# Choosing the experts ahead of the second softmax, splitting all expert weights in the value stage, and weighting the expert outputs as they are added

## What is computed

```
logits = jnp.mean(x, axis=1) @ Wr + br                    # one row per image
routing_weights = jax.nn.softmax(logits, axis=-1)
scale = jnp.where(expected_loads > capacity, capacity / expected_loads, 1.0)
routing_weights = jax.nn.softmax(routing_weights * scale, axis=-1)
top_w, top_i = jax.lax.top_k(rw_tok, K)                   # the same for every token of an image
top_w = jax.nn.softmax(top_w, axis=-1)
h = jax.nn.gelu(jnp.einsum('nd,edf->enf', xf, W1) + b1[:, None, :], approximate=False)
y = jnp.einsum('enf,efd->end', h, W2) + b2[:, None, :]
out = jnp.einsum('ne,end->nd', w_dense, y).reshape(B, S, D)
out = _layer_norm(out + x, gamma, beta)
```

## Time and profile before

| what | value |
|---|---|
| time, median of 3 runs | 410.57 us (410.19 to 412.47) |
| span of the profiled execution, first to last instruction | 408.4 us |
| own time of the profiled execution | not given apart from its span; the median lies 2.2 us above the span |
| mean granted TensorE clock | 0.995 |
| busy: PE, DVE, ACT, POOL | 391.0, 311.4, 279.5, 116.5 us |
| shares of the chain that ended last | PE 83%, DVE 7%, ACT 4%, issue 3%, DMA 2% |

### The profile page before, as it was taken

How to read it: one execution, slowest core, us unless ns; L and a number is a source line. 1 busy time by engine, 2 the same in 40 slices (tenths; PEclk the granted TensorE clock), 3 DMA queues, 4 the chain that set the end, 5 groups by cost and what they waited for, 6 DMA issues and landing times.

```text
span 408.4 us, 5562 instructions
## 1 busy us (share of the span) xinstructions
PE 391.0 (96%) x1887; PEld 302.0 (74%) x1892; DVE 311.4 (76%) x699; ACT 279.5 (68%) x530; POOL 116.5 (29%) x113
## 2 busy tenths in 40 slices
PE   8899898999999999999999899999999999998994
PEld 3579895688777888888886688888887766645772
DVE  3798935768888988988899798898899265557745
ACT  1566654558598888888877788888888201457980
POOL 8200004440430730332132063574320000224015
PEclk9999999999999999999999999999999999999999
DMA  7990000000000000000000180000000000000002
GB/s 274 383 312 2 2 2 0 1 2 0 2 1 0 2 0 1 2 1 2 0 0 2 71 343 2 0 0 2 1 1 2 0 2 0 0 2 1 0 2 103
DMA packets 5262, 15.51 MB, mean 38 GB/s; under 512 B 690, under 2 KB 1906, under 8 KB 4978
## 3 DMA queue, kind: packets, MB, share of 16 engines
q1 hardware_dynamic: 4802, 14.19, 9.3%
q10 hardware_dynamic: 432, 0.97, 0.6%
HBM read 14.08 MB, written 1.08 MB: 37 GB/s over the span
## 4 chain that ended last, share of the span: by engine, by line
PE 83%; DVE 7%; ACT 4%; issue 3%; DMA 2%; DVEq 0%; SPq 0%; ACTq 0%
PE ps L1066 13%; PE ps L1068 13%; PE ps L1067 13%; PE ps L1050 13%; PE ps L1162 7%; PE ps L970 2%; PE ps L1002 2%; PE ps L1009 2%; DMA xq<-laid_x_queries 2%; DVE nmax_all L1520 2%; PE ps L827 2%; PE ps L936 2%; PE ps L912 2%; PE ps L959 1%; PE ps L990 1%
## 5 line engine op out<-in xcount | busy, mean ns | idle before, releaser
L706 ACT ACTIVATE exps<-ps,nmax_all 128x1024 bf16<-128x1024 f32 x128 | 142.8, 1115 | 32.5 <-DVE diag_all L1525 32.0
L1520 DVE TENSOR_REDUCE nmax_all<-ps 128x1 f32<-128x1024 f32 x128 | 156.6, 1224 | 7.1 <-PE ps L1068 5.5
L1066 PE MATMUL ps<-qT_hi,kT_hi 128*128 128x512 f32 x256 | 104.7, 409 | 2.2 <-ACT a_rows L723 1.1
L1068 PE MATMUL ps<-qT_hi,kT_lo 128*128 128x512 f32 x256 | 99.8, 390 | 0.0
L1067 PE MATMUL ps<-qT_lo,kT_hi 128*128 128x512 f32 x256 | 99.7, 390 | 0.0
L1066 PEld LDWEIGHTS ps<-qT_hi,kT_hi 128*128 128x128 f32 x256 | 48.1, 188 | 15.6 <-ACT exps L706 1.8
L1050 PE MATMUL ps<-xn,wqkv 128*128 128x342 f32 (+3 forms) x256 | 58.2, 379 | 0.0
L1067 PEld LDWEIGHTS ps<-qT_lo,kT_hi 128*128 128x128 f32 x256 | 48.1, 188 | 10.8 <-issue 0.2
L1068 PEld LDWEIGHTS ps<-qT_hi,kT_lo 128*128 128x128 f32 x256 | 48.0, 188 | 10.3
L487 POOL CAST qT_hi<-xq 128x1024 fp32r<-128x1024 f32 x15 | 15.6, 1040 | 132.5 <-ACT xq L696 132.5
L1050 PEld LDWEIGHTS ps<-xn,wqkv 128*128 128x128 f32 x256 | 42.6, 189 | 11.6 <-issue 1.2
(11 more groups left out here) (216 smaller groups left out, 560.2 us busy)
## 6 DMA issues: line engine op xcount, KB each, us to landing
xs_first<-a_store SPq DMA_DIRECT2D x4, 512.0 KB, 5.4
xs_second<-a_store SPq DMA_DIRECT2D x4, 512.0 KB, 8.3
wqkv<-laid_qkv_weights SPq DMA_DIRECT2D x1, 1536.0 KB, 6.2
wvT<-laid_qkv_weights_T SPq DMA_DIRECT2D x1, 1536.0 KB, 9.5
xq<-laid_x_queries SPq DMA_DIRECT2D x2, 512.0 KB, 6.2
xk<-laid_x_keys SPq DMA_DIRECT2D x2, 512.0 KB, 7.8
x<-in_x SPq DMA_DIRECT2D x1, 1024.0 KB, 12.5
w<-in_L_ffn_W SPq DMA_DIRECT2D x1, 1024.0 KB
```

The lines of the kernel that those rows point to most:

```text
L706: a.activation(exps[:, n % 2, :], slot(job_slot(("score", u, n))), ACT.Exp, bias=nmax_all[:, col:col + 1], accum_out=sum_all[:, col:col + ...
L1066: mm(tgt, keys_hi, qT_hi[:, u % 2, at], start=True, stop=False)
L1068: last = mm(tgt, keys_lo, qT_hi[:, u % 2, at], start=False, stop=True)
L1520: v.tensor_reduce(nmax_all[:, col:col + 1], slot(place), AX_X, ALU.max, negate=True)\
```

## The change

Five things are changed.

- The router takes `max` and `max_index` from the scaled weights, ahead of the second softmax, whose order is the same. The second softmax goes on with its maximum taken from `max`. The gates are made from a hyperbolic tangent of half the difference; the Gelu table is loaded before it.
- POOL splits W1 and W2 of all eight experts in the value stage, once the score job two from the end is done: two copies and two subtractions of 128 x 2048 each. The room is that of tensors no longer needed (`x`, `wqkv`).
- After the indices POOL copies, for each pair, the first bias, hi and lo of W1, hi and lo of W2 and the second bias. `second_layer` on DVE goes.
- W2 no longer carries the gate. Each step's output has a bank of its own (three in turn) and DVE adds it as bank times gate plus running sum, eight times in place of four.
- The gated second bias is added to the tokens by POOL, chunk by chunk, after its copies; DVE's first addition of a chunk waits for it.

```diff
@@ pool, between the attention units and xn_lo @@
+            pool.wait_ge(ffn_in, 64)
+            pool.wait_ge(job_ps, len(JOBS) - 2)
+            pool.wait_ge(w2_centred, E)
+            g.tensor_copy(w1_all_hi[:, :, :], w1[:, :, :]).then_inc(w_rounded, 1)
+            g.tensor_copy(w2_all_hi[:, :, :, :], w2[:, :, :, :]).then_inc(w_rounded, 1)
+            pool.wait_ge(w_rounded, 2)
+            g.tensor_tensor(w1[:, :, :], w1[:, :, :], w1_all_hi[:, :, :].bitcast(F32), ALU.subtract)\
+                .then_inc(w_rounded, 1)
+            g.tensor_tensor(w2[:, :, :, :], w2[:, :, :, :], w2_all_hi[:, :, :, :].bitcast(F32), ALU.subtract)\
+                .then_inc(w_rounded, 1)
+            pool.wait_ge(w_rounded, 4)
...
+            pool.wait_ge(xs_used, UNITS)
+            pool.wait_ge(t1_beta, 2)
+            pool.wait_ge(b2_centred, 1)
             pool.wait_ge(idx_ready, 2)
...
-                    g.tensor_copy(w1_hi[:, b, k, :], chosen).then_inc(w1_ready, 1)
-                    pool.wait_ge(w1_ready, 2 * n + 1)
-                    g.tensor_tensor(w1_lo[:, b, k, :], chosen, w1_hi[:, b, k, :].bitcast(F32), ALU.subtract)\
-                        .then_inc(w1_ready, 1)
+                    g.tensor_copy(b1s[:, b, k, :], b1_all[:, bass.ds(e, 1), :].rearrange("p o f -> p (o f)"))\
+                        .then_inc(b1_ready, 1)
+                    for table, to in ((w1_all_hi, w1_hi), (w1, w1_lo)):
+                        g.tensor_copy(to[:, b, k, :], table[:, bass.ds(e, 1), :].rearrange("p o f -> p (o f)"))\
+                            .then_inc(w1_ready, 1)
+                    for table, to in ((w2_all_hi, w2_hi), (w2, w2_lo)):
...
+                    g.tensor_copy(b2s[:, b, k:k + 1], b2c[:, bass.ds(e, 1)]).then_inc(b2_ready, 1)
+            pool.wait_ge(b2_ready, 2 * TOPK)
+            pool.wait_ge(gates_ready, TOPK)
+            for k in range(TOPK):
+                g.tensor_tensor(b2g[:, :, k], b2s[:, :, k], rs_[:, 10 + k, :], ALU.mult).then_inc(b2_scaled, 1)
+            pool.wait_ge(b2_scaled, TOPK)
+            step(g.tensor_tensor(b2sum[:, :], b2g[:, :, 0], b2g[:, :, 1], ALU.add))
+            for c in range(4):
+                at = slice(c * 512, (c + 1) * 512)
+                g.tensor_scalar(xn[:, at], xn[:, at], b2sum[:, c // 2:c // 2 + 1], None, ALU.add).then_inc(xn_biased, 1)
@@ act, router @@
+            load_table(ACT.Gelu)
             act.wait_ge(r_in, 3)
-            a.activation(rs_[:, 8, :], rs_[:, 7, :], ACT.Exp).then_inc(r_exp, 1)
-            load_table(ACT.Gelu)
+            a.activation(rs_[:, 8, :], rs_[:, 7, :], ACT.Tanh, scale=0.5).then_inc(r_exp, 1)
...
-                act.wait_ge(w2_ready, 4 * (b * TOPK + k) + 1)
+                act.wait_ge(b1_ready, b * TOPK + k + 1)
@@ pe @@
-            for signal, count, times in ((r_exp, 2, 6), (r_in, 2, 4), (r_exp, 4, 4), (idx_ready, 2, 6)):
+            for signal, count, times in ((r_exp, 2, 6), (r_in, 2, 2), (idx_ready, 2, 6)):
...
-                pe.wait_ge(w2_ready, 4 * (b * TOPK + k) + 4)
-                if k == 0 and c >= 2:
-                    pe.wait_ge(LN[2]["centred"], c - 1)
+                pe.wait_ge(w2_ready, 2 * (b * TOPK + k) + 2)
+                if n >= 3:
+
+                    pe.wait_ge(first_added if (n - 3) % 2 == 0 else LN[2]["centred"], (n - 3) // 2 + 1)
@@ dve @@
-            softmax_input(rt[:, 5, :, :], 3)
-            softmax_output(4, 6, 7, 4)
...
+                v.max(rt[:, 8, b, :], rt[:, 5, b, :]).then_inc(dve_step, 1)
...
+            v.tensor_scalar(rs_[:, 3, :], rt[:, 8, :, 0], -1.0, None, ALU.mult).then_inc(r_in, 1)
...
+                v.max_index(top_i[:, b, :], rt[:, 8, b, :], rt[:, 5, b, :]).then_inc(idx_ready, 1)
...
-            second_layer(0)
...
+            def add_output(n):
+
+                c, k = n // 2, n % 2
+                at = slice(c * 512, (c + 1) * 512)
+                dve.wait_ge(y_ps, n + 1)
+                if k == 0:
+                    dve.wait_ge(xn_biased, c + 1)
+                else:
+                    dve.wait_ge(first_added, c + 1)
+                v.scalar_tensor_tensor(centred[:, at], bank(y_bank(n)), rs_[:, 10 + k, c // 2:c // 2 + 1],
+                                       (centred if k else xn)[:, at], ALU.mult, ALU.add)\
+                    .then_inc(LN[2]["centred"] if k else first_added, 1)
+
+            dve.wait_ge(gates_ready, TOPK)
             hidden_remainder(0)
             hidden_remainder(1)
-            second_layer(1)
...
+            for n in range(8):
+                if n == 6:
                     reciprocals(2, 0)
-                residual(c)
...
+                add_output(n)
+                if n + 2 < 8:
+                    hidden_remainder(n + 2)
             reciprocals(2, 1)
```

More of the change, by code:

```diff
@@ L120, in build @@
         head_sel = sb("head_sel", [9 * HEADS, HEADS, P], BF16)
-        x = sb("x", [P, N])
+        with ExitStack() as before_attention:
+            x = before_attention.enter_context(nc.sbuf_tensor("x", [P, N], F32))
+        w1_all_hi = sb("w1_all_hi", [P, E, FF], F32R)
         conv_wT = sb("conv_wT", [P, 3, C])
@@ L135, in build @@
         bqkv = cols[:, NROWS:NCOLS].rearrange("p (j h) -> p j h", j=3)
-        wqkv = sb("wqkv", [P, HEADS, 3, D])
+        with ExitStack() as attention_weights:
+            wqkv = attention_weights.enter_context(nc.sbuf_tensor("wqkv", [P, HEADS, 3, D], F32))
+        w2_all_hi = sb("w2_all_hi", [P, E, FC, D], F32R)
+        w1_lo = sb("w1_lo", [P, 2, TOPK, FF], F32R)
         bqkv_q = sb("bqkv_q", [P, 3, HEADS])
@@ L238, in build @@
         b2s = sb("b2s", [P, 2, TOPK])
+        b2g = sb("b2g", [P, 2, TOPK])
         hid = conv_o[:, :].rearrange("p (n f c) -> p n f c", n=2, f=FC)
@@ L1254, in outputs @@
                     pe.wait_ge(h_lo, 2 * n + f + 1)
-                    tgt = bank(4 + c % 2)
-                    mm(tgt, w2_hi[:, b, k, f, :], hid_hi[:, n % 2, f, :], start=(k == 0 and f == 0), stop=False)
+                    tgt = bank(y_bank(n))
+                    mm(tgt, w2_hi[:, b, k, f, :], hid_hi[:, n % 2, f, :], start=f == 0, stop=False)
                     mm(tgt, w2_hi[:, b, k, f, :], hid_lo[:, n % 2, f, :], start=False, stop=False)
                     last = mm(tgt, w2_lo[:, b, k, f, :], hid_hi[:, n % 2, f, :], start=False,
-                              stop=(k == 1 and f == FC - 1))
+                              stop=f == FC - 1)
                 last.then_inc(y_ps, 1)
@@ L1670, in _ @@
-            v.tensor_tensor(rs_[:, 7, :], rt[:, 8, :, 1], rt[:, 8, :, 0], ALU.subtract).then_inc(r_in, 1)
-            dve.wait_ge(r_exp, 5)
[L1672 to L1687, removed]
-                    v.tensor_scalar(b2s[:, b, k:k + 1], b2c[:, bass.ds(e, 1)], rs_[:, 10 + k, b:b + 1], None,
-                                    ALU.mult).then_inc(w2_ready, 1)
-                    dve.wait_ge(w2_ready, 4 * n + 3)
-                    v.scalar_tensor_tensor(lo_, chosen, rs_[:, 10 + k, b:b + 1], hi_.bitcast(F32),
-                                           ALU.mult, ALU.subtract).then_inc(w2_ready, 1)
-                dve.wait_ge(w2_ready, 4 * (b + 1) * TOPK)
-                step(v.tensor_tensor(b2sum[:, b:b + 1], b2s[:, b, 0:1], b2s[:, b, 1:2], ALU.add))
@@ L1715, in hidden_remainder @@
                                     ALU.subtract).then_inc(h_lo, 1)
-            def residual(c):
-                dve.wait_ge(y_ps, 2 * c + 2)
-                v.scalar_tensor_tensor(centred[:, c * 512:(c + 1) * 512], bank(4 + c % 2),
-                                       b2sum[:, c // 2:c // 2 + 1], xn[:, c * 512:(c + 1) * 512], ALU.add, ALU.add)\
-                    .then_inc(LN[2]["centred"], 1)
+            def add_output(n):
[10 more added lines that the diff above has]
+            dve.wait_ge(gates_ready, TOPK)
             hidden_remainder(0)
             hidden_remainder(1)
-            second_layer(1)
-            for c in range(4):
-                if c < 3:
-                    hidden_remainder(2 * c + 2)
-                else:
+            for n in range(8):
+                if n == 6:
                     reciprocals(2, 0)
-                residual(c)
-                if c < 3:
-                    hidden_remainder(2 * c + 3)
+                add_output(n)
+                if n + 2 < 8:
+                    hidden_remainder(n + 2)
             reciprocals(2, 1)
@@ L1736, in _ @@
             lay_diagonal(2, 3, last_diagonal)
-            normalise_last(0, 1)
-            normalise_last(1, 2)
-            normalise_last(2, 3)
-            normalise_last(3, 4)
+            for c in range(4):
+                normalise_last(c, LAST_SPREAD[c])
             dve.wait_ge(LN[2]["out"], 4)
```

47 lines of the change are left out of this document (28 added, 19 removed).

## The result

The changed kernel took 416.91 us (median; 415.92 to 417.10) beside 410.38 (409.29 to 412.47) for the kernel before in the same comparison: a ratio of 1.0141 with an interval of 1.0112 to 1.0169. The profiled execution has a span of 415.4 us (417.1 us in all) against 408.4, a granted clock of 0.991 against 0.995, and 140.2 us of POOL in place of 116.5. The four executions have spans of 414.2 to 415.4 us.

The account below looks back on a forecast made before the run. PE bounds the value stage and most expert steps, DVE and ACT the router, DVE the end. 5.0 + 1.2 - 2.6 + 0.8 + 0.65 = 5.05 us on 410.57 gives 415.6; range 408.9 to 417.2, forecast's own 413.2 to 417.0.

Parts of the forecast that it names:

- PE's gap before the turn: Value stage: PE idles before the turn of image 1's weights, waiting for DVE's pieces; cost 5.0 us, bounds 0 to 6.0.
- clock: Value stage, behind PE's idle stretch: the granted clock falls and PE runs slower; cost 1.2 us, bounds 0 and 1.5.
- first steps: First expert steps: without `second_layer` on DVE, the third Gelu step starts at 374.0 instead of 376.66; gain 2.6 us.
- bias late: Expert stage: POOL's first biased chunk comes at 376.5, needed by 375.7, delaying PE's outputs(2); cost 0.8 us, between 0 and 2.3.
- the end: Last chunks: one addition more on DVE stands ahead of the last square; cost 0.65 us, bounds 0.6 and 0.75.
- Part 1: Split in the value stage: POOL's two long subtractions hold DVE's two-input sums, so PE waits 5.0 us, plus 1.2 for clock.
- Parts 2 and 3: Router and W2 off DVE: hidden(0) starts 1.7 us earlier, the third Gelu step at 374.0; gain 2.6 us together.
- The rival of Tanh with tables of its own: Before the first Gelu: Tanh needs two more table loads, first steps 2.2 us later; 417.0 us in all, chance 0.10.
- Part 4: Bias on POOL, expert stage: DVE's first `add_output` waits for POOL's first biased chunk, delaying outputs(2); cost 0.8 us.
- The rival that POOL's copies bound the first steps: Expert stage: POOL's copies at 0.465 each and exposed value loads add 1.5 us; 417.1 us in all, chance 0.08.
- Part 5: End of the kernel: `reciprocals(2, 0)` stands ahead of two additions, so the last square waits for one more; cost 0.65 us.
- The rival "not held": Value stage: DVE slips in between POOL's reads, PE's turn stays at 321.28; 409.4 us in all, not slower, chance 0.32.

## Why the prediction was right

It said 415.6 us, slower, by a named mechanism; the time is 416.91 and the mechanism is the one named. The time alone would not have told: two of the rivals, at 417.0 and 417.1, lie nearer to it, and it stands only 0.1 us under the upper end of the forecast's own range, as four of the five terms were put too low. (The lower end, 413.2, adds up to 413.4 from the terms that it names.) The measured terms beside its steps:

| step | predicted | in the trace |
|---|---|---|
| PE's gap before the turn | 5.0 | 4.75 |
| clock | 1.2 | 1.79 |
| first steps | -2.6 | -2.5 |
| bias late | 0.8 | 1.7 |
| the end | 0.65 | 0.87 |
| ahead of the value stage | none | 0.41 |
| sum | 5.05 | 7.0 |

**Part 1.** The subtractions took 4.52 and 4.50 us (predicted 4.6). Net of the 0.41, L1579 ended at 319.71 (predicted 319.7), L1593 at 324.17 (324.3), and the turn came at 326.03 (326.25). A copy took 1.90 us; the prediction wrote 1.9, though its price for each element makes 1.8. What carried this was the earlier trace rows: 16 elements that waited out a POOL subtraction. That row has one input in SBUF, so it is of the kind of the casts and not, as the prediction said, of L1538; the sum at 404.06 in the same rows is of its kind. The earlier trace rows pointed the other way, and both ways are found. Beside POOL's copies and subtractions it goes by who began first: they hold DVE, and a copy that comes second waits (0.86 us in place of 0.40 at 377.52, behind the remainder of 377.24). The Trainium skill's rule ("SBUF — State Buffer", section "Who interferes with whom") says so, and these rows agree with it in both directions. Beside POOL's addition of one operation the measurement differs from that rule: the remainder of 371.73 began second and wasn't held, and POOL paid. In the kernel before, the sum just ahead of those in the earlier trace rows also began second, by 0.10 us:

```profile
61.65 0.96 POOL L463 TENSOR_SCALAR conv_e<-conv_e,st 128x336 f32<-128x336 f32 x1
61.75 0.53 DVE L1440 TENSOR_TENSOR x<-x,conv_e 128x352 f32<-128x352 f32 x1 [0.82 <-ACT conv_e L652]
```

It took 0.53 us, and POOL 0.96 where the instruction before it had taken 0.63. Why these POOL instructions give way no run shows. The Trainium skill's rule agrees in a further point that the prediction didn't take up: the same section counts casts among the DVE instructions that can take the shared ports, and L1588 and L1592 were held, at 0.70 to 1.18 us.

**The clock** is a term that was mis-sized: 1.79 us, more than the 1.2 taken and beyond the bound of 1.5. (0.16 of it is the turn's own start behind a gap: with the subtractions in pieces it took 0.61 us in the chain too, at a clock of 1.00. That leaves 1.63.) The step that failed is "some of the low stretch will lie inside the gap": the granted clock was 1.00 through the gap to 326 and at the lower level (0.50) on the work behind it, so PE paid for nearly all of it. In the run of the split alone 0.7 us did lie inside the gap, but the low stretch was longer and cost 3.17 us. The bound came from "three microseconds" of the earlier trace rows and was too tight for those rows too: at means of 0.76 and 0.54 on either side of two stretches at 0.50 the low stretch adds up to 0.48 + 2 + 0.92 = 3.4 us, half of which is 1.7.

**Parts 2 and 3** came as said. Shifted by 6.95, POOL's first copy starts at 366.87 (predicted 366.9), hidden(0) at 367.79 (367.8), the first Gelu at 368.85 (368.9), the third Gelu step at 374.16 (374.0). The rival of Tanh with tables of its own is false: the one load before Gelu at 373.22 is followed by the hyperbolic tangent at 374.62, 0.19 us long, with no other load. The list in the Trainium skill ("ScalarE: Activation LUTs", section "Table sets: the hidden batching unit") doesn't name tanh for gelu's set; on this chip it was served without a load.

**Part 4** is the term that was mis-sized most. The bias was there 1.15 us later than predicted (384.60 - 6.95 = 377.65 in place of 376.5). Of that, 0.83 is the addition: 1.58 us where the prediction had taken 0.75, carried on from the 128x256 product of the earlier trace rows, which has two operations; the two-operation form of the same 512 elements takes 0.69. The other 0.32 is POOL's copies and small steps, among them copies that waited for a remainder of DVE's: 0.86 us in place of 0.40 at 377.52. The cost at `outputs(2)` is 2.5 - 0.77 = 1.7 us, inside the bounds of 0 to 2.3; over the whole stage the bias by image gave back 2.1. One of the prediction's own signs of being wrong, `add_output(0)` waiting for POOL by far more than a microsecond, was there: DVE stood idle for 2.86 us before it, and PE for 1.68 before `outputs(2)`. The rival that POOL's copies bound the first steps (417.1) was right that this term could be larger, but not in its reason: undisturbed, the copies started 0.34 us apart, less than the 0.42 taken; the addition was the slow part.

**Part 5** is off in size alone: the two last additions stand 0.82 us apart in the chain, not 0.63, and the end cost 0.87 (0.89 given back).

**The rival "not held"** named 409.4 us for parts 2 to 5 without the stall. The kernel with the earlier split is that case, at 410.48: with the bias at 1.7 and the end at 0.87 its sum would have been 410.57 - 2.5 + 1.7 + 0.87 = 410.6.

What stays open: why the clock fell at different moments behind the same gap and stayed low for longer in one execution, and why POOL's addition of one operation is slow and lets DVE through.

## What to carry to other kernels

Moving work to an idle POOL isn't free while DVE makes short sums or casts out of SBUF: look at what DVE does in that stretch, put long POOL instructions beside DVE work that reads PSUM (the maxima kept their 1.22 us), or cut them into short ones, so that a wait is a piece and not the whole (a gap of 0.58 us in place of 4.76). When PE's idle gap is filled with matmuls that do nothing, the clock after it is kept, which gave back 2.2 us here. And of work that several consumers wait for, do first what the first consumer needs: a bias added image by image, the same work in another order, made the stage 2.1 us shorter.

## What was not expected of the hardware

- One form of a POOL instruction can cost twice another: adding a column to 128x512 took 1.58 us as one operation, 0.69 us with a product by one behind it. The slow form left DVE's two-input remainder its 0.69 us and took 2.10 itself; beside the quick form the remainder took 1.11.
- DVE's casts of 192 elements, with one input in SBUF, waited for POOL like the two-input sums: 0.33 us alone, 0.77 beside subtractions of 0.71 us, 1.18 beside copies of 1.04 us. The reciprocal took 0.54 to 0.55 in all three places, beside POOL each time.
- Behind the same gap in PE's work the clock's price isn't the same in each execution. After 4.76 us it fell as the work came back, and cost 1.79 us; after 4.77 us, in the run of the split alone, it had fallen 0.7 us ahead of the work, and cost 3.17 us. Behind the gap of 0.58 us it didn't fall (1.00 from 321 to 326).
